# Pair tables computed in the attention stage, and the routing of the last two batches half a period earlier

## What is computed

```
xn = layernorm(x)
s  = attention(xn @ WQ, xn @ WK, xn @ WV)            # causal, one head of 256
f  = mixture(xn)                                     # over all 4096 tokens
out = x + s * silu(f)
```

```
scores  = softmax(xf @ w_gate.T)
groups  = top 2 of 4 groups of (scores + expert_bias)
topk_idx, weights = top 2 experts in those groups    # weights are the plain scores
flat_idx = topk_idx.reshape(-1)
routed_in = xf[flat_idx] * weights
h = silu(grouped(routed_in, w1, counts)) * grouped(routed_in, w3, counts)
out = shared.at[flat_idx].add(grouped(h, w2, counts))
```

## Time and profile before

| | |
|---|---|
| median of 3 runs | 238.85 us (238.68 to 239.2) |
| profiled execution | 240.62 us, its span 238.6 us |
| TensorE busy | 230.6 us (97%), 1533 products |
| VectorE busy | 186.8 us (78%) |
| ScalarE busy | 144.9 us (61%) |
| GpSimd busy | 55.4 us (23%) |
| chain that ended last | TensorE 92% of the span, line 392 alone 85% |

### The profile page before, as it was taken

How to read it: one execution, slowest core, us unless ns; L and a number is a source line. 1 busy time by engine, 2 the same in 40 slices (tenths; PEclk the granted TensorE clock), 3 DMA queues, 4 the chain that set the end, 5 groups by cost and what they waited for, 6 DMA issues and landing times.

```text
span 238.6 us, 4677 instructions
## 1 busy us (share of the span) xinstructions
PE 230.6 (97%) x1533; PEld 205.8 (86%) x1533; DVE 186.8 (78%) x620; ACT 144.9 (61%) x392; POOL 55.4 (23%) x108
## 2 busy tenths in 40 slices
PE   7898999999999999999999999999999999999983
PEld 5788998998989989999899998898988889898843
DVE  3779859989899899897977985677776867869765
ACT  2444745755648457474574723779678696878722
POOL 5220631805509136073012000002020201202000
PEclk9999999999999999999999979999999999999999
DMA  5699420020200200000000000116847557393523
GB/s 156 207 326 304 157 91 1 1 87 5 88 3 0 88 3 3 0 3 0 0 3 1 0 3 0 48 26 196 142 105 197 76 145 122 103 199 57 140 74 102
DMA packets 18758, 19.45 MB, mean 82 GB/s; under 512 B 1064, under 2 KB 17712, under 8 KB 18736
## 3 DMA queue, kind: packets, MB, share of 16 engines
q1 hardware_dynamic: 15568, 16.02, 21.4%
q0 software_dynamic: 3168, 3.15, 9.1%
HBM read 14.95 MB, written 4.21 MB: 80 GB/s over the span
## 4 chain that ended last, share of the span: by engine, by line
PE 92%; DMA 2%; DVE 2%; ACT 1%; issue 1%; SPq 1%; DVEq 0%; ACTq 0%
PE bank L392 85%; PE bank L484 4%; PE bank L440 3%; DMA raw_qkv<-in_L_attn_WK 2%; DVE raw_sw L1382 1%; DVE w L1380 1%; PE bank L556 1%; PE bank L414 0%; SPq L220 0%; DVE arena L949 0%; ACT xT_hi_all L731 0%; ACT arena L731 0%; ACT probs L731 0%; ACT attn_all L731 0%; SPq L222 0%
## 5 line engine op out<-in xcount | busy, mean ns | idle before, releaser
L392 PE MATMUL bank<-xT_hi_all,arena 128*128 128x512 f32 (+3 forms) x256 | 80.7, 370 | 0.7 <-DVE arena L949 0.7
L392 PE MATMUL bank<-arena 128*128 128x256 f32 (+2 forms) x560 | 76.8, 285 | 0.3 <-ACT attn_all L731 0.3
L392 PEld LDWEIGHTS bank<-arena 128*128 128x128 f32 (+1 forms) x560 | 71.9, 186 | 5.0 <-issue 0.8
L392 PEld LDWEIGHTS bank<-xT_hi_all,arena 128*128 128x128 f32 x256 | 47.0, 189 | 8.3 <-ACT probs L761 1.4
L731 ACT ACTIVATE arena<-bank 128x512 fp32r<-128x512 f32 (+4 forms) x84 | 36.2, 452 | 24.4 <-PE bank L392 23.1
L949 DVE TENSOR_TENSOR arena<-bank,arena 128x264 fp32r<-128x264 f32 (+4 forms) x83 | 41.4, 508 | 6.9 <-ACT arena L731 6.0
L392 PE MATMUL bank<-xT_lo_all,arena 128*128 128x512 f32 (+3 forms) x128 | 45.8, 358 | 0.0
L383 POOL DMA_DIRECT2D x_ring<-in_L_attn_x x6 | 7.9, 1317 | 79.0 <-DVE x_ring L1318 79.0
L392 PEld LDWEIGHTS bank<-xT_lo_all,arena 128*128 128x128 f32 x128 | 24.2, 189 | 2.1
L731 ACT ACTIVATE attn_all<-bank,row_inv 128x256 f32<-128x256 f32 x32 | 15.2, 474 | 17.3 <-PE bank L392 15.5
L761 ACT ACTIVATE probs<-bank,neg_max 128x128 f32<-128x128 f32 (+3 forms) x32 | 17.0, 530 | 12.6 <-DVE neg_max L1008 12.5
(11 more groups left out here) (128 smaller groups left out, 381.9 us busy)
## 6 DMA issues: line engine op xcount, KB each, us to landing
x_ring<-in_L_attn_x SPq DMA_DIRECT2D x7, 512.0 KB, 3.5
x_ring<-in_L_attn_x POOLq DMA_DIRECT2D x6, 512.0 KB, 6.0
out<-x_ring SPq DMA_DIRECT2D x6, 512.0 KB, 3.3
spread<-pairs SPq DMA_DIRECT2D x14, 128.0 KB, 3.3
w_sb<-in_L_ffn_w SPq DMA_DIRECT2D x1, 1024.0 KB, 11.9
raw_sw<-in_L_ffn_sw SPq DMA_DIRECT2D x3, 256.0 KB, 4.2
x_ring<-in_L_attn_x SPq DMA_DIRECT2D x2, 256.0 KB, 2.9
xn<-in_L_attn_x SPq DMA_DIRECT2D x1, 512.0 KB, 5.3
```

Source lines behind the costliest of these rows:

```text
L392: return nc.tensor.matmul(dst, lhsT, rhs, start=start, stop=stop, skip_group_check=True, **kw)
```

## The change

It has five parts.

1. **Tables in the first stage.** In the periods of batches 2 to 5 `tables(n)` stands between `turn_probs(b, 0)` and `scores(b, 2)` on TensorE. The weights are split like all else and are now the moving operand (256 columns, two experts), and the high and low parts of the first eight tokens (`first8`, 16 columns) are stationary. Eight products a period, 32 in all; the result has 16 rows, one set of eight from the high tokens and one from the low.
2. **Their feeding.** ScalarE copies the high part of the weights (`table_high`, two of 512 columns a period) and keeps the result (`table_keep`); GpSimd subtracts for the low part (`table_low`); SyncE writes the tables to DRAM and reads them back with one row per pair; GpSimd adds the two halves in batch 6's period and, with ScalarE, splits A. `table_bank`, `xn8`, `A_T`, `B_T` and the transpose of A are gone.
3. **Routing.** The last 8 of the 20 steps of batch 6 stay in the last attention and the first 12 move into batch 6's own period; of batch 7's steps the first 9 move from behind the last attention into it, 11 stay behind.
4. **Start of the second stage.** All eight table calls go. `hidden(0, 0, 0)` stands ahead of `weigh(7, 3)`, the three others of batch 7 behind it, then the counting, `hidden(1, 0, 0)`, and the routing products and gathers with nothing between them. ScalarE's order follows.
5. **Tail.** VectorE multiplies the reduced sums by B (64 rows, 128 columns) ahead of the last transpose; the multiply behind it becomes a copy.

```diff
@@ TensorE, first stage
+            def tables(n):
+                pe.wait_ge(s["first8_ready"], 2)
+                pe.wait_ge(s["v_lo"], T * (n + TABLES + 1))
+                for u in range(2):
+                    pe.wait_ge(s["table_lo"], 2 * n + u + 1)
+                    w = w_split[:, u, :, :].rearrange("p h (e c d) -> p h e c d", e=2, c=C)
+                    for c in range(C):
+                        for h in range(2):
+                            ins = mm(v_bank[0:16, u * D:(u + 1) * D], first8[:, c, :], w[:, h, :, c, :], c == 0 and h == 0, c == C - 1 and h == 1)
+                ins.then_inc(s["tables_summed"], 1)
...
                 turn_probs(b, 0)
+                if TABLES <= b < TABLES + 4:
+                    tables(b - TABLES)
                 scores(b, 2)
@@ TensorE, last attention and start of the second stage
             turn_sw(2)
-            table(0, 0)
             weigh(b, 0)
             turn_probs(b, 2)
-            table(0, 1)
             weigh(b, 1)
             turn_probs(b, 3)
-            table(0, 2)
             weigh(b, 2)
-            table(0, 3)
-            weigh(b, 3)
...
-            pe.wait_ge(s["a_split"], 2)
-            nc.tensor.transpose(x_bank[0][:, 0:P], A_T[:, :].bitcast(F32), ident[:, :]).then_inc(s["a_turned"], 1)
-            table(1, 0)
             pe.wait_ge(s["sw_ready"], 3)
             pe.wait_ge(s["exp_done"], T * B)
             hidden(0, 0, 0, h1_bank, "h1_done")
-            table(1, 1)
+            weigh(b, 3)
+            hidden(0, 1, 0, h1_bank, "h1_done")
+            pe.wait_ge(s["pT_lo"], T * B)
+            hidden(0, 0, 1, h3_bank, "h3_done")
+            hidden(0, 1, 1, h3_bank, "h3_done")
             pe.wait_ge(s["route"], ROUTED)
...
-            pe.wait_ge(s["pT_lo"], T * B)
-            hidden(0, 0, 1, h3_bank, "h3_done")
-            table(1, 2)
+            hidden(1, 0, 0, h1_bank, "h1_done")
             pe.wait_ge(s["rows_ready"], 1)
             turn_pairs()
             spread_pairs(0)
-            hidden(0, 1, 0, h1_bank, "h1_done")
             pe.wait_ge(s["a_ready"], 1)
             gather(0, 0)
             spread_pairs(1)
+            gather(0, 1)
             pe.wait_ge(s["pairs_kept"], 1)
-            table(1, 3)
-            hidden(0, 1, 1, h3_bank, "h3_done")
-            gather(0, 1)
@@ ScalarE
+            def table_high(n, u):
...
+                copy(w_split[:, u, 0, :], table_weights(2 * n + u)).then_inc(s["table_hi"], 1)
+            def table_keep(n):
...
+                copy(table_cols.rearrange("p e d -> p (e d)"), v_bank[0:16, :]).then_inc(s["tables_kept"], 1)
...
             silu_hidden(0, 0)
+            silu_hidden(0, 1)
+            h_high(0, 0)
             act.wait_ge(s["pairs_turned"], 1)
             copy(pair_T[:, :], acc_bank[0:NR, 3 * P:4 * P]).then_inc(s["pairs_kept"], 1)
-            h_high(0, 0)
             silu_rows(0, 0)
-            silu_hidden(0, 1)
             rows_high(0, 0)
+            h_high(0, 1)
             silu_rows(0, 1)
-            h_high(0, 1)
             rows_high(0, 1)
@@ GpSimd
+                nc.gpsimd.tensor_tensor(w_split[:, k % 2, 1, :], table_weights(k), w_split[:, k % 2, 0, :].bitcast(F32),
+                                        ALU.subtract).then_inc(s["table_lo"], 1)
@@ VectorE, start of the second stage
+            routes(b, 9, ROUTE)
+            h_mult(0, 0)
...
             pair_one_hots(0, 0)
-            h_mult(0, 0)
             one_hot(0, 0)
+            h_mult(0, 1)
             one_hot(0, 1)
             h_low(0, 0)
-            dve.wait_ge(s["tables_summed"], 8)
-            nc.vector.tensor_copy(B_T[:, :], bank[7][:, 0:PAIRS]).then_inc(s["b_kept"], 1)
-            h_mult(0, 1)
             rows_low(0, 0)
             h_low(0, 1)
@@ VectorE, tail
-                                    AX.X, ALU.add).then_inc(s["sum_ready"], 1)
+                                    AX.X, ALU.add).then_inc(s["sum_part"], 1)
+            dve.wait_ge(s["b_ready"], 1)
+            dve.wait_ge(s["sum_part"], 1)
+            nc.vector.tensor_tensor(sum_w[0:PAIRS, :], sum_w[0:PAIRS, :], B_rows[:, :], ALU.mult).then_inc(s["sum_ready"], 1)
             dve.wait_ge(s["sum_turned"], 1)
-            nc.vector.tensor_tensor(pair_out, bc_bank[:, 0:PAIRS], B_T[:, :], ALU.mult).then_inc(s["pairs_ready"], 1)
+            nc.vector.tensor_copy(pair_out, bc_bank[:, 0:PAIRS]).then_inc(s["pairs_ready"], 1)
```

More of the change, by code:

```diff
@@ L132, in build @@
         swT = part(SW).rearrange("p (h w c d) -> p h w c d", h=2, w=3, c=C)
-        A_stack = part(P)
         assert part_end[0] <= XT + VV // 2
@@ L176, in build @@
         largest = scratch(T)
+        A_sum = scratch(H)
+        assert scratch_end[0] <= 3 * C * D
         e_of = sb("e_of", [P, NT, K])
@@ L445, in values @@
                 dst = v_bank
+                if t == 0 and TABLES < b <= TABLES + 4:
+                    pe.wait_ge(s["tables_kept"], b - TABLES)
                 if b == 0:
@@ L1198, in _, with routes @@
                 step(b)
-            step(B - 2, norm=False)
+            def routes(b, first, end):
+                for k in range(first, end):
+                    route(b, k)
+            b = B - 2
+            p = b + 1
+            row_max(b, 0)
+            logits_max(b)
+            routes(b - 1, 0, 2)
+            row_max(b, 1)
+            routes(b - 1, 2, 4)
+            x_low(p, 0)
+            routes(b - 1, 4, 6)
+            x_low(p, 1)
+            p_low(b, 0)
+            logits_sum(b)
+            routes(b - 1, 6, 8)
+            row_max(b, 2)
+            logits_inv(b)
+            routes(b - 1, 8, 11)
+            v_low(p, 0)
+            routes(b - 1, 11, 13)
+            invert(b, 0)
+            invert(b, 1)
+            routes(b - 1, 13, 15)
+            p_low(b, 1)
+            routes(b - 1, 15, 17)
+            row_max(b, 3)
+            routes(b - 1, 17, 18)
+            v_low(p, 1)
+            routes(b - 1, 18, 20)
+            p_low(b, 2)
+            routes(b, 0, 2)
+            q_low(p, 0)
+            routes(b, 2, 3)
+            invert(b, 2)
+            v_low(p, 2)
+            routes(b, 3, 4)
+            p_low(b, 3)
+            routes(b, 4, 6)
+            invert(b, 3)
+            routes(b, 6, 7)
+            q_low(p, 1)
+            routes(b, 7, 8)
+            v_low(p, 3)
+            routes(b, 8, 12)
             b = B - 1
```

185 lines of the change are left out of this document (104 added, 81 removed).

## The result

The changed kernel takes 245.31 us (243.94 to 246.6, 4 runs), the kernel before beside it 239.02 us (238.68 to 239.24, 4 runs): ratio 1.0258, 95% interval 1.0226 to 1.029. It is slower, as forecast, but the range of 240.0 to 243.4 us doesn't hold it. The profiled execution took 246.27 us, span 244.2.

What follows compares the result with a forecast made beforehand. TensorE was taken to bound the kernel. First stage +3.8, start of second stage -2.2 and tail +0.3 made +1.9; a returning low clock of 1.0 made +2.9 on the 238.85 us median: 241.7 us, range 240.0 to 243.4.

Steps and rivals of the forecast that it cites:

- idle time of about 3 us: Last attention: TensorE idles about 3 us in place of 2.4 us of table work, so removing three calls gains nothing.
- the routing chain: Start of second stage: steps from counting at 145.6 to the low half of the hidden tile at 154.3 us.
- rival 3: First stage: VectorE in batch 6's period or GpSimd's subtractions become the bound, 243 to 244.5 us; chance 0.07.
- Rival 4: Last attention: three table calls were on the path, 2.4 us less, 239.3 us; chance 0.07 shared with shorter waits.
- I take 1.0: After the last attention's idle time: a returning low-clock stretch costs 1.0 us, from a span of 0.9 to 1.7.
- The low clock costs half of 3.4 us, 1.7: Around 139.5 to 142.9 us before the change: 1.7 us of low-clock cost, counted among 5.8 us leaving TensorE.
- the net of the start of the second stage: First batch's shared output starts at 154.3 instead of 156.56 us: -2.2 us, with 0.4 either way.
- the sum without any low clock: Whole kernel: +3.8 first stage, -2.2 start of second stage, +0.3 tail, giving +1.9 us.
- rival 1: Last attention: no low-clock stretch comes back, 240.8 us (240.4 to 241.2); chance 0.28.
- Table products in the first stage: Batches 2 to 5: 32 products at 0.12 us add 3.8 us, all on TensorE's path.
- What feeds them: First stage: ScalarE's copies and GpSimd's subtractions fit in free time, covered by 0.9 us or more; cost nothing.
- Tail: Ahead of the last transpose: VectorE's new 64x128 multiply, with TensorE waiting, costs 0.3 us; the later copy nothing.

Runs made afterwards that it cites:

- `route_only`: Kernel before with only the routing steps moved half a period forward, its table calls kept: 238.93 us, ratio 0.9984.
- `five_calls`: Kernel before without its first three table calls (table A incomplete): five of twelve runs at full clock took 238.61 to 239.13 us, six 242.2 to 242.7, one 248.28.
- `fill_both`: Changed kernel with unused products filling TensorE's waits in both the last attention and the routing: 241.88 us, ratio 1.0106.
- `small_low`: Changed kernel with GpSimd's subtraction cut from 512 columns to 8, all 32 table products kept (tables wrong): 243.27 us, ratio 1.0183.
- `few_tables`: Changed kernel with 8 of the 32 table products in the first stage (tables incomplete): 243.62 us, ratio 1.0154.
- `order_late`: `order` with the routing steps back in their old places: 240.48 us, ratio 1.0051.
- `order`: Changed kernel with hidden groups and counting moved into TensorE's waits, ScalarE's and VectorE's lists reordered to match: 235.84 us, ratio 0.9855.

## Why the prediction was right and wrong

**Right:** that it is slower; the two waits of the last attention (1.7 and 1.1 us, 2.8 in all, "idle time of about 3 us") and that the three calls ahead of them are worth nothing in time; that the routing chain takes 8.7 us from the counting to the low half (8.8 measured, 150.85 to 159.67); that the earlier routing is unused (through at 142.6 us, taken up at 150.85; `route_only`); that batch 6's period isn't held, against half of rival 3 (15.35 us, 113.84 to 129.19, and 15.38 before); that the clock falls. Rival 4 is refuted by `five_calls`. One sign didn't show: the longest wait of the routing was to be for the low half of the hidden tile, and in the changed kernel there is none, as the last hidden group ran at the low clock past it; in `fill_both` it is 0.54 us. The waits of the routing were 2.6 us (0.51, 0.94 and 1.14), not 3.7.

**The step that failed: the size of the low clock, "I take 1.0".** It assumed one stretch as long as the one seen, 3.4 us, and nothing of a second. The profile has two of 6.8 us, costing 2.66 and 2.14. The bound of "0.9 to 1.7, second 0 to 0.8" came from a single row of before, which showed one length; it said nothing of how long a stretch gets where more idle time stands around it. Rows of the routing chain said that TensorE would wait 3.7 us there, more than in the last attention, and that alone should have put a second stretch of full cost into the range. Of the 3.6 us between the forecast and the measured median this step is 2.4: at the median the low clock cost 3.4 us (245.31 less 241.88), where 1.0 was taken.

**The second fault: base and sum were on different footings.** "The low clock costs half of 3.4 us, 1.7" was counted as leaving the kernel and taken off the profiled execution, and the sum was then added to the median. The profiled execution was 1.8 us above the median, and just this stretch was the difference. Against the median the net of the start of the second stage is -0.5, not -2.2, and the sum without any low clock +3.6, not +1.9. `fill_both` shows +2.9, so the sum without low clock was off by only 1.0. That is luck: table products taken 0.7 us too dear hid part of the 1.7 (1.9 + 1.7 - 0.7 + 0.1 of the tail is 3.0). For the same reason rival 1, with 240.8 us, is too low even for a run with no dip. With the low clock as it was in the profile (+4.8) this gives 239.0 + 2.9 + 4.8 = 246.7; measured 246.27.

**Table products in the first stage, "3.8 us, all of it on the path".** It was 3.1. The price per product was nearly right (0.124 for 0.12), but the 15.40 of 15.40 us of TensorE in the earlier trace rows held about 0.2 us a period in which it could take more work (0.61 us between starts where 0.43 is enough, above). The ends of products are modelled, so a row that reads as busy need not be at its rate.

**What feeds them, "nothing".** The cover of 0.9 us was read for GpSimd alone, and its subtractions took 1.27 instead of 1.04 us. What was missed is who else stands beside it: VectorE's step on `gs` starts at 81.31, 0.1 us behind the first subtraction, and ends at 82.57, 0.1 us after it (82.48); the next one starts at 83.02 and ends at 83.80, 0.1 us after the second (83.72). So VectorE is held until GpSimd is done, about 1.6 us more a period for the two steps. Its step between them (L1063, 82.49 to 82.77, one input in PSUM) took its usual 0.28 us beside the second subtraction. The Trainium skill (SBUF — State Buffer, SBUF: two separate sides) states it so: a VectorE operation with two inputs in SBUF and a GpSimd operation that reads SBUF exclude each other, and the later one waits for the whole of the other. By that rule a step of 0.21 us that starts beside a subtraction ends only behind it, and the trace agrees (1.26, 0.78, and 0.21 again once the subtraction is short). It changed no time here only because TensorE was just as late (`small_low`). Rival 3 had named the subtractions, for their own lateness and not for this.

**Tail:** 0.3 taken, 0.39 measured (0.97 less 0.58).

## What to carry to other kernels

Before work that fills a wait is taken out, ask what else will fill it. Here three of the calls cost no time where they stood, and the waits that the new order left open cost 2.1 to 4.7 us by the clock alone. Filling them with products that nobody uses gave that back, and filling them with the next stage's own products made 1.0258 of the kernel before into 0.9855. Dips came and went from run to run of one kernel, so one profile with or without a dip says little about its cause: compare the clocks of all runs. Check whether the profiled execution is a typical one (its time and granted clock against the runs) before a term is taken from a part in which the clock is low. And a step moved ahead off the path is worth nothing until what it waits behind moves too: cost it in the order that you will end with.

## What the runs showed of the hardware that was not expected

- The granted clock fell with no long idle time: in the changed kernel after a wait of 1.71 us and inside one of 1.14, with 1.4 us of work between them. In `few_tables` and `small_low` it didn't fall at the same two waits. In `order_late` it fell 1.2 us after work had begun again behind a wait of 2.72 us. In `order`, with 0.33 us, it stayed up in all six runs.
- The dips in the kept profiles were about 3.4 or 6.8 us long, in `five_calls` once some 20 us (137 to 157 us), and which one comes differs from run to run of one kernel: 243.94 to 246.6 us for the changed kernel, 238.61 to 248.28 for `five_calls`. In the profiles a mean clock of 0.992 or 0.993 goes with one dip of 3.4 us, 0.986 with one of 6.8.
- A 128x64 step of VectorE with its two inputs in SBUF took 0.21 us alone and 1.26 and 0.78 us beside GpSimd's subtractions of 128x512. These took 1.27 to 1.29 us, all eight of them, however long the step stood beside them, where the operations of 128x512 in the earlier trace rows took 1.04; that VectorE lengthened them isn't shown.
